# Scores in 64x64 tiles, v and the router's logits in one product, earlier score units and a later selection in an attention and mixture-of-experts block

## What is computed

```python
xn = layernorm(x)
q, k, v = split(xn @ w_in.T + b_in)                 # 16 heads of 8
scores = einsum('bhqd,bhkd->bhqk', q * scale, k) + causal_bias
out = softmax(scores) @ v                           # heads side by side
out = out @ w_out.T + b_out; out = where(isnan(out), 0, out)
s = softmax(xn @ gate_w.T)                          # 8 experts
w, i = top_k(s, 2); w = w / (w.sum(-1) + 1e-20) * 2.5
g = silu(xn @ w_gate[e]) * (xn @ w_up[e])           # 176 columns an expert
y = sum_e combine[:, e] * (g @ w_down[e])           # combine holds w at i
shared = silu(xn @ sw_gate) * (xn @ sw_up) @ sw_down
x = x + out + y + shared
```

## Time and profile before

| | |
|---|---|
| median of 3 runs | 625.84 us (625.79 to 627.24) |
| the profiled execution | 626.86 us, its span 625.1 us |
| busy: PE, DVE, ACT, POOL | 553.6, 466.0, 346.0, 352.3 us |
| weight loads (PEld) | 311.6 us |
| granted TensorE clock | 0.97 over the span |
| chain that ended last | PE 66%, DVE 12%, issue 7%, ACT 5% |

### The profile page before, as it was taken

The page is one execution under the profiler, slowest core; times in us unless marked ns, Lnnn a source line. Parts: engine busy times, 40 slices in busy tenths (PEclk is TensorE's granted clock), DMA queues, the critical chain, the costliest instruction groups (busy, mean ns, idle before and its releaser), DMA issues.

```text
span 625.1 us, 12489 instructions
## 1 busy us (share of the span) xinstructions
PE 553.6 (89%) x4144; PEld 311.6 (50%) x4144; DVE 466.0 (75%) x781; ACT 346.0 (55%) x472; POOL 352.3 (56%) x357
## 2 busy tenths in 40 slices
PE   1336999999999999999999999999999999999884
PEld 1223664466525664466535664466534664366421
DVE  3974887589785997589775997589776997489602
ACT  1511349733794349733794349733794349733591
POOL 3332764468454764468454774568454774468442
PEclk9757999999999999999999999999999999999897
DMA  5928103540037003450037102450047002450000
GB/s 142 315 60 192 37 1 105 151 138 18 29 126 196 40 17 105 140 146 17 19 134 195 42 17 104 133 154 17 9 144 202 35 17 104 137 152 18 4 2 17
DMA packets 42854, 56.71 MB, mean 91 GB/s; under 512 B 4400, under 2 KB 28304, under 8 KB 42704
## 3 DMA queue, kind: packets, MB, share of 16 engines
q1 hardware_dynamic: 42832, 56.43, 31.0%
HBM read 41.21 MB, written 14.81 MB: 90 GB/s over the span
## 4 chain that ended last, share of the span: by engine, by line
PE 66%; DVE 12%; issue 7%; ACT 5%; SPq 4%; DMA 4%; POOL 1%; POOLq 0%; DVEq 0%; ACTq 0%
PE banks L579 10%; PE banks L450 7%; PE banks L452 6%; PE banks L451 6%; PE banks L552 6%; PE banks L479 6%; PE banks L461 5%; ACT probs L769 5%; PE banks L470 4%; DVE neg_max L1077 4%; PE banks L463 3%; PE banks L462 3%; DMA cb<-c_dram 2%; DVE max_parts L1097 2%; DVE probs L1059 1%
## 5 line engine op out<-in xcount | busy, mean ns | idle before, releaser
L1077 DVE TENSOR_REDUCE neg_max<-banks 128x2 f32<-128x1024 f32 (+3 forms) x224 | 194.6, 914 | 33.7 <-PE banks L470 32.9
L832 POOL TENSOR_TENSOR probs<-probs,cb 128x512 f32<-128x512 f32 x88 | 115.7, 1315 | 77.0 <-ACT probs L721 72.9
L769 ACT ACTIVATE probs<-banks 128x1024 f32<-128x1024 f32 x160 | 154.2, 1032 | 8.6 <-PE banks L552 7.0
L865 POOL TENSOR_SCALAR_AFFINE_SELECT probs<-probs 128x512 f32<-128x512 f32 x128 | 93.3, 749 | 100.0 <-ACT probs L769 99.7
L838 POOL TENSOR_TENSOR hid_lo<-probs,hid_hi 128x512 fp32r<-128x512 f32 (+1 forms) x88 | 112.9, 1284 | 64.9 <-ACT hid_hi L728 64.9
L721 ACT ACTIVATE probs<-banks 128x512 f32<-128x512 f32 (+1 forms) x112 | 66.9, 598 | 143.5 <-PE banks L452 142.2
L1059 DVE TENSOR_TENSOR probs<-probs,banks 128x512 f32<-128x512 f32 (+1 forms) x112 | 75.5, 680 | 34.3 <-PE banks L452 15.1
L450 PE MATMUL banks<-x_hi,w_hi 128*128 128x512 f32 (+1 forms) x224 | 94.1, 420 | 4.5 <-DVE w_lo L1212 2.7
L728 ACT ACTIVATE hid_hi<-probs 128x512 fp32r<-128x512 f32 (+1 forms) x112 | 70.3, 628 | 47.7 <-DVE probs L1059 46.6
L579 PE MATMUL banks<-probs,v_op 128*32 128x512 f32 (+3 forms) x1024 | 95.2, 444 | 0.3
L452 PE MATMUL banks<-x_hi,w_lo 128*128 128x512 f32 (+1 forms) x224 | 89.5, 399 | 0.0
(11 more groups left out here) (114 smaller groups left out, 602.0 us busy)
## 6 DMA issues: line engine op xcount, KB each, us to landing
cb<-c_dram SPq DMA_DIRECT2D x32, 256.0 KB, 4.5
q_op<-q_dram SPq DMA_DIRECT2D x32, 192.0 KB
k_op<-k_dram SPq DMA_DIRECT2D x32, 192.0 KB
cb<-c_dram SPq DMA_DIRECT2D x16, 224.0 KB, 4.6
q_dram<-q_parts SPq DMA_DIRECT2D x8, 384.0 KB, 2.5
k_dram<-k_parts SPq DMA_DIRECT2D x8, 384.0 KB, 2.5
cb<-c_dram SPq DMA_DIRECT2D x16, 192.0 KB, 4.3
cb<-c_dram SPq DMA_DIRECT2D x16, 160.0 KB, 4.6
```

Of the source, the lines that this page charges most:

```text
L769: nc.scalar.activation(probs[:, g % 2, 2 * u:2 * u + 2, :], ring[:, at:at + 2, :], ACT.Exp).then_inc(exp_done, 1)
L832: nc.gpsimd.tensor_tensor(sg[k % 3][:, :], sg[k % 3][:, :], cb[:, TILE_ORDER[k], :], ALU.mult).then_inc(weighted, 1)
L865: return nc.gpsimd.affine_select(out=view, in_=view, compare_op=ALU.is_ge, fill=0.0, base=0, pattern=[[0, 4], [1, P]], channel_multiplier=-1)
L1077: return nc.vector.tensor_reduce(out, in_, AX.X, ALU.max, negate=True)
```

## The change

The heads' matmuls and the masks' are cut into column halves, so that four tiles of 64 by 64 work side by side (c is the half of the query rows). The mask's second half needs only the last 64 columns, and a mask is one round instead of two that add halves of the identity. v and logits become one product over 136 columns into banks 4 and 5; q goes to bank 5, one exponential sooner. The router's weights are transposed at once, 32 rows by 128. Units 0 and 1 move to the end of the attention, all others one or two steps forward, and seven units share one buffer. The final selection moves to step 14, ahead of the last hidden product, and the first exponential waits for that product, since it overwrites what the selection reads. The transfer of the maxima goes ahead of the store; a new semaphore, base_free, guards base.

```diff
-PAIRS_AT = [int(k in (1, 11)) + 2 * int(2 <= k <= 10) for k in range(NT + 2)]
-ONE_SLOT = 5
+PAIRS_FIRST = [2 * int(2 <= k <= 11) for k in range(NT + 2)]
+PAIRS_AT = [int(k in (0, 10)) + 2 * int(1 <= k <= 9) for k in range(NT + 2)]
+ONE_SLOT = 7
...
+        vl = banks[:, 4:6, 0:2 * (E + NE)].rearrange("p a (b c) -> p a b c", b=2)
+        q_bank = banks[:, 5, :]
...
             def maxima_in(b):
                 sp.wait_ge(mrows_done, b + 1)
-                before(sp, stored, 16 * b)
...
                 operands_in(i + 1, i, 1)
+                maxima_in(i + 1)
                 store(i)
-                maxima_in(i + 1)
+                sp.wait_ge(stored, 16 * i + 16)
+                apart(sp, base_free)
...
+            def project_v_and_logits(j):
                 pe.wait_ge(xnT_done, j + 1)
                 before(pe, mrows_done, j)
                 for q in range(QT):
-                    mm = pe.matmul(bank_m[:, q * NE:(q + 1) * NE], xnT[:, q * P:(q + 1) * P], gate_sb[:, :],
+                    mm = pe.matmul(vl[:, q // 2, q % 2, :], xnT[:, q * P:(q + 1) * P], wvg_sb[:, :],
                                    start=True, stop=True)
...
-                for q in range(QT):
-                    mm = pe.transpose(bank_m[0:NE, q * P:(q + 1) * P], comb[:, q, :], ident_sb[:, :])
-                mm.then_inc(combT_ready, 1)
+                pe.transpose(bank_m[0:QT * NE, 0:P], comb[:, :, :].rearrange("p q e -> p (q e)"), ident_sb[:, :]
+                             ).then_inc(combT_ready, 1)
...
+            def mask_scores(bank, a, c, at, stride, nblk):
                 own = slice(HALF * a, HALF * (a + 1))
+                cols = slice(at % stride + HALF * c, at % stride + P)
+                blocks = bank[HALF * c:HALF * (c + 1), a, :].rearrange("p (k n) -> p k n", n=stride)
+                return pe.matmul(blocks[:, at // stride:at // stride + nblk, cols], ident_half[own, :],
+                                 mask_half[own, 0:P - HALF * c].unsqueeze(1).to_broadcast([HALF, nblk, P - HALF * c]),
+                                 start=False, stop=True, tile_position=(HALF * a, HALF * c), skip_group_check=True)
...
                 for m, (j, qt, at) in enumerate(parts):
-                    for a in range(2):
-                        head_scores(bank, a, 4 * g + j + a, qt, at, m == 0)
-                for last in range(2):
+                    for c in range(2):
+                        for a in range(2):
+                            head_scores(bank, a, c, 4 * g + j + a, qt, at, m == 0)
+                for c in range(2):
                     for a in range(2):
-                        mm = mask_scores(bank, a, *masks, last)
+                        mm = mask_scores(bank, a, c, *masks)
...
                         if front and g == GROUPS and u in (2, 3):
+                            pair(i + 1, i, u - 2)
                             gate_up(i + 1, u - 2)
...
+                        if n == 0:
+                            act.wait_ge(hid_done, NT * i + NT)
...
+                    if k == NT and i is not None:
+                        find_numbers(i)
+                        finish_output(i)
                     if k >= 1:
                         hidden(b, k - 1)
...
-                    if k == 6 and i is not None:
-                        find_numbers(i)
-                    if k == 8 and i is not None:
-                        finish_output(i)
...
                 if front:
+                    take_v(i + 1)
                     split_k(i + 1)
-                    take_v(i + 1)
                     split_q(i + 1)
```

More of the change, by code:

```diff
@@ L161, in block_kernel @@
         after = 2 * FT + NT * E
-        mask_f = early[:, after:after + 2 * P].rearrange("p (a n) -> p a n", a=2)
-        ident_f = early[:, after + 2 * P:after + 4 * P].rearrange("p (a n) -> p a n", a=2)
+        mask_f = early[:, after:after + P]
+        ident_f = early[:, after + P:after + P + HALF]
         att = probs[:, 0, 0, :].rearrange("p (q e) -> p q e", q=QT)
@@ L257, in block_kernel @@
         summed = sem("summed")
+        base_free = sem("base_free")
         stored = sem("stored")
@@ L617, in experts_and_maxima @@
                         transpose_o(i, 1)
-                    late = int(k < 4 and PAIRS_AT[k] > 1)
-                    for _ in range(PAIRS_AT[k] - late):
+                    ahead = int(k < EARLY and i is not None)
+                    late = int(2 <= k < 4)
+                    for _ in range(pairs_at[k] - ahead - late):
                         pair(b, i, n)
@@ L630, in experts_and_maxima @@
                         down(b, k - 2, i)
+                    if k == 2 and i is not None:
+                        transpose_on(i)
+                    if k == 3 and i is not None:
+                        project_out(i)
                     for _ in range(late):
@@ L637, in experts_and_maxima @@
                         transpose_maxima(b)
-                    if k == 2 and i is not None:
-                        transpose_on(i)
-                    if k == 3 and i is not None:
-                        project_out(i)
             def attend(i, front):
@@ L648, in attend @@
                         if front and (g, u) == (0, 2):
-                            project_q(i + 1)
-                        if front and (g, u) == (0, 3):
-                            project_v(i + 1)
+                            project_q(i + 1, q_bank)
                         if (g, u) == (0, 3):
@@ L665, in _ @@
             transpose_x(0)
-            logits(0)
-            project_q(0)
+            project_v_and_logits(0)
+            project_q(0, bank_y)
             project_k(0)
-            project_v(0)
             transpose_comb(0)
```

109 lines of the change are left out of this document (52 added, 57 removed).

## The result

The changed kernel took 633.5 us (median of 4 runs, 632.4 to 634.4) against 626.5 in the same series: a ratio of 1.0105, 95% interval 1.0079 to 1.013. It is about 7 us slower, where 621.9 was forecast, and it lies above the range. In the profiled executions the spans are 630.7 and 625.1 us, 5.6 apart. I measure the *period* from the first gate product of tile 4 in one block to that of the next, as the mean of the four periods from the third block on: 70.53 us before, 71.26 now.

The account below looks back on a forecast made before the run. ScalarE paces attention, TensorE the tile steps with VectorE close behind, a latency chain the block's end. Attention -4.4, block ends +1.5, last block -0.7, start -0.4 make -4.0: 626.86 to 622.9, median 1.0 lower, 621.9 us; range 614 to 630.

Parts of the forecast that it names:

- From the last exponential to tile 12: First tiles, tile steps and stall up to tile 12: it would start at 228.45.
- The waits of units 4 and 7: First tiles: unit 4 waits for unit 3's maxima, +0.5 us, unit 7 for the attention's sum, +0.35.
- Tiles 4 to 9: Tile steps: smaller masks cut a step from 3.20 to 3.05 us, with VectorE's 3.0 fitting under it.
- The rival of short rounds that wait: Score units: rounds of four tiles cost 0.03 us each, perhaps load waits too; 630.7 to 635 us, chance 0.16.
- End of the block: Tile 12 onward: a chain of latencies through splitting, hidden and down products leaves down 11 where it was, at 234.37.
- most of those 4.1 us is lost: End of block: unit 19 starts 4.1 us sooner, but splitting holds up hidden 10, so tile 12 waits 1.7 us.
- The new wait of the first exponential for the last hidden product costs nothing: Start of attention: that product ends near 236.0, before the exponential's old start at 237.3, so cost 0.
- The final selection (1.4 us) falls into VectorE's idle time before that product: End of block: the selection's 1.4 us on VectorE fits ahead of the last hidden product without cost.
- over 1 us later: Start of attention: only if GpSimd were this late would the first exponential's new wait cost time.
- Attention: Seven attention stretches: no separate v and one router transpose close ScalarE's gaps, -0.63 us each, -4.4 in all.
- Last stretch: Last block, without v and x and gated by the maxima: -0.7 us.
- The end of the block stretches: Rival, tiles 10 to 13: GpSimd or ScalarE late by 0.5 us more, eight times, giving 625.9 us; chance 0.13.

Follow-up runs that it names:

- E4: E3 with the splitting of the maxima also moved, to behind the hidden product of tile 10; 615.6 us.
- E3: The changed kernel with the final selection one step sooner, at step 13, ahead of the hidden product of tile 12; 627.2 us.
- E9: The changed kernel with score units, output transposes and buffers back in the order of before, selection still late; 619.2 us.
- E5: The changed kernel without the two operations of the final selection, the attention's part left out of what is stored; 625.3 us.
- E13: The changed kernel with only the test of equality moved sooner, behind the hidden product of tile 12, the copy staying in step 14; 626.0 us.
- E2: The kernel before with only the final selection moved to step 14, and what this needs; 633.0 us.
- E1: The changed kernel with the final selection put back in steps 6 and 8; 633.3 us.
- E14: E10 with the whole final selection, test and copy, moved behind the hidden product of tile 12; 634.3 us.
- E15: E9 with the whole final selection, test and copy, moved behind the hidden product of tile 12; 633.3 us.
- E10: The changed kernel with only the splitting of the maxima moved, to behind the hidden product of tile 10; 620.0 us.

## Why the prediction was wrong

- *From the last exponential to tile 12: right in sum.* Last exponential to tile 12: 41.61 us before, 41.30 now, -0.31; forecast -0.32 (228.45 against 228.77). The waits of units 4 and 7 came at 0.42 and 0.45 (forecast +0.5 and +0.35).
- *Tiles 4 to 9: right.* 3.01 us a step on average, forecast 3.05; the tiles take what the masks save, 1.59 us in 18 units of a period or 0.088 a unit. The rival of short rounds that wait, which had the chance of the slower side, did not happen. It was priced at 630.7 to 635, and the 633.5 falls there by coincidence.
- *End of the block: right up to down 11*, which I had at 234.37 and is at 234.13. But "most of those 4.1 us is lost" was taken as given, where it was worth a step of its own: the stall of tile 12 that I computed cost 1.8 us a period (E4 against E3), and with the units left in their places the kernel would have won 7 us (E9).
- **The step that failed**: "The new wait of the first exponential for the last hidden product costs nothing" and "The final selection (1.4 us) falls into VectorE's idle time before that product". The idle time was there, 1.52 us, and it was GpSimd's weighing that VectorE waited for in it (timeline of VectorE, kernel before):

```profile
230.37 1.28 DVE L1097 CAST max_parts<-max_rest 128x64 bf16<-128x64 f32 x1
231.69 0.23 DVE L1099 TENSOR_TENSOR max_parts<-max_rest,max_parts 128x64 bf16<-128x64 f32 x1
...
235.84 0.69 DVE L1059 TENSOR_TENSOR probs<-probs,banks 128x512 f32<-128x512 f32 x1 [1.52 <-POOL probs L832]
```

  I set 1.4 us of durations into a gap of 1.5 without asking what GpSimd does in it. The test was held until the weighing ended, and the pair ended 1.5 us behind it. I had even named the case "over 1 us later", for GpSimd alone. That the exponential waits for the product is not the cost by itself: E5 and E13 keep that wait. The selection in that place costs 0.98 us a period (E5), forecast 0.
- *Attention: right in kind, too large.* Forecast -0.63 us a stretch; first to last exponential is 19.96 where down 12 isn't late (E5), against 20.35: -0.39. In the changed kernel itself it is 20.24, as the late down 12 takes 0.28 of it. The gaps of 0.25 and 0.18 closed; that of 0.24, of which I expected 0.20, stayed as it was. From the fifth exponential to the nineteenth the stretch even takes 14.05 us where it took 13.73, and fifteen run at 14.71 / 15 = 0.98 us each where ten took 0.955; why was not followed up. ScalarE in the changed kernel:

```profile
242.38 14.71 ACT L775 ACTIVATE probs<-banks 128x1024 f32<-128x1024 f32 x15
257.33 1.94 ACT L775 ACTIVATE probs<-banks 128x1024 f32<-128x1024 f32 x2 [0.24 <-PE banks L556]
```

- *Last stretch: wrong.* Forecast -0.7, measured +2.5: one more wait of 1.29 us, and a granted clock of 0.50 for 10 us instead of 3.5. I had not asked where one more wait could cost clock as well.
- *The sum.* Forecast -0.38 us a period. Without the selection it was 70.27 - 70.53 = -0.26. With 0.98 on it +0.72. The -0.26 is near partly by luck: the attention brought 0.24 less than forecast, and from last to first exponential it was +0.11 where the forecast had +0.25, as the product of v and logits took 1.02 us and not 1.14.
- *The rivals.* "The end of the block stretches" named the right place and sign, with GpSimd or ScalarE late, at 0.5 us and 0.13; it was VectorE, held by GpSimd, at twice that. Two operations moved into a chain of which I said that it has no slack; priced at the length of one weighing, 1.28 us in eight blocks, this rival would have come to 632.

What I could have used: the Trainium skill, SBUF — State Buffer, section Who interferes with whom, says that a VectorE instruction with two inputs in SBUF and a GpSimd instruction that reads SBUF exclude each other for their whole length, and that whichever starts first blocks the other. The runs agree: 1.77 us against 0.68 for the test. The trace of before had the like for the casts (above): 64 columns took 1.28 us beside GpSimd, whose weighing ran from 230.33 to 231.60, and the subtraction of the same size behind it 0.23.

## What to carry to other kernels

Before moving a VectorE operation into a gap, look at what GpSimd does in that gap: if it is GpSimd that VectorE waits for there, an operation with all its operands in SBUF may be held until GpSimd is done, and what VectorE still has to do then stands in front of what it waited for. Here 0.2 us of start decided which of the two was held (0.08 behind in the changed kernel, 0.13 ahead in E2), and both cost time, 0.98 and 0.66 us a period. When one edit makes units ready sooner, move at once what stands behind the last of them (here four small operations ahead of a hidden product), or the gain turns into a stall. Weigh an edit with the others on: the tiles were worth 0.55 us a period alone and 1.59 beside the rest, and taking the selection out of the steps paid only with them.

## What was not expected of the hardware

- Two engines hold each other off in both directions: the test 1.77 us instead of 0.68 when it began 0.08 us after the weighing; the weighing 1.69 instead of 1.28 when the test began 0.13 us before it (E2). The predicated copy is held in the same way, 1.83 instead of 0.73 (E13). The hidden product, with one input in PSUM, isn't: 0.68 us on average, with GpSimd at work or not.
- A held operation of any size can last over 1 us: casts and subtractions of 64 columns took up to 1.3 us beside GpSimd and 0.2 otherwise (the splitting's first subtraction 1.24 us on average in E1 and its second cast 0.20; in the changed kernel 0.35 and 1.04).
- TensorE's granted clock fell to 0.50 (1.2 GHz) behind some idle times of 1.3 to 2.4 us, and not behind others of the same length. Behind one of 2.14 us (2.42 in the last block) it fell in six of seven blocks (E14), behind one of 2.26 in two of seven (E15), behind one of 1.57 in two of seven (E1), and behind the wait of 1.51 us for tile 12 in the changed kernel in none. Each of these falls lasted some 3.5 us. The pair of 1.3 us in the last block was followed by 10 us in the changed kernel and by 3.5 in E10. The wait of 0.89 us left it at 1.00. A single trace thus doesn't tell what a wait costs in clock; the share of the blocks in which it falls tells more.
